# A decoder block whose attention computes its scores a second time with the keys as rows, instead of transposing the probabilities

## The chip, the cores and the metric

The kernel runs on one core of one Trainium2 chip. The metric is the device time of one execution in microseconds. Three runs of the kernel before gave a median of 816.69 us (815.62 to 818.06).

## The reference, cut to what matters

```
x = x + attn(layernorm(x))              # 4 x 512 x 512, 16 heads of 32, causal
x = x + xattn(layernorm(x), ctx, ctx)   # queries = layernorm(x), keys = values = ctx, causal
x = x + ffn(layernorm(x))
attn:  q, k, v = x @ w.T + b;  softmax(mask(q k' / sqrt(32))) @ v;  then @ o_w.T + o_b
ffn:   relu(x @ W_up.T) @ W_down.T + sum(softmax(top2(x @ W_gate.T))) * (x @ W_expert)
```

Everything is fp32. The softmax subtracts the largest score of its row.

## The kernel before, in words

Each engine runs one list of instructions, written out in the order of a loop over steps `s`; every step has 8 slots `i` (`z = 8 s + i`). A step handles one pair of heads. There are 32 pairs of self attention (4 batch entries of 8) and then 32 of cross attention; two pairs make a group `G` of four heads, 128 columns of the model. The order is the same on all engines, and engines meet through semaphores only.

Large matmuls are made exact enough by splitting each operand in a high and a low part (fp32r) and adding three products, lines 412 to 414. One such filling of a bank is 12 matmuls of 512 columns ("a fill"): Q, K of each group, V and O of each batch entry, and FG, FU, FE, FD of the feed-forward part. `plan` (line 91) lists the fills by slot, one quarter of a fill per slot, and gives each one of two banks. Fills of the feed-forward part of batch entry f begin at slot `FEED[f]`, steps 42.5, 51.5, 60 and 67.5.

For the scores the three products lie one above the other in a `stack` tile of 96 rows (32 numbers per head, three times), which SyncE fills by six DMAs per pair from `stage` (line 278), two steps ahead of use. Then, per pair, for each of two heads and each of four blocks of 128 queries:

- TensorE: `scores` (line 370), one matmul with queries as rows, 128 to 512 keys wide, because the mask is causal; three banks take turns.
- VectorE: `top_of` (line 558) adds the mask, scales, writes the tile to SBUF and takes the row's negative maximum.
- ScalarE: `exped` (line 770), the exponential with that maximum as bias and with the row sum accumulated.
- In self attention VectorE takes the reciprocal of four row sums (line 572) and GpSimd multiplies the tile by it (line 872).
- TensorE: `turn` (line 382), 20 transposes of 128x128 per pair, so that keys are rows; ScalarE (line 779) and VectorE (line 568) copy them out of two banks into `prob`.
- Every second step `values` (line 406): 16 matmul calls, each 32 columns of V against up to 512 columns of `prob`, four side by side in the array. Each call shows as two instructions.

In cross attention the division comes later: the result is transposed back (`back`, line 513) and multiplied by the reciprocal of the sums (`back_scaled`, line 681). At step s the engines work on the scores of pair s+1, the turning of pair s, and at even s the values of group s/2-1.

Of the kernel before, what the change touches and what calls it, by code (L numbers as in the profile page):

```python
# [59 lines left out]
FIRST = -4  # L60
# [5 lines left out]
NS, NTB = 3, 2  # L66


FEED = (PAIRS * 42 + 4, PAIRS * 51 + 4, PAIRS * 60, PAIRS * 67 + 4)


def feed_start(f):

    return FEED[f]


def stats_step(j):

    return PAIRS * (j - 1) + (2 if j == B + 2 else 0)


def norm_slots(j):

    z = PAIRS * PAIRS * (j - 1) + PAIRS * (2 if j < B else 3)
    return [z + 4, z + 5, z + 8, z + 9] if j == B + 2 else [z, z + 1, z + 4, z + 5]


END = (feed_start(B - 1) + UNITS) // PAIRS + 1


def plan():
# [6 lines left out]
    for G in range(NGS):  # L98
        put(("Q", G), 2 * G - 4, 4 if G and G % KC == 0 else 0, 4)
        put(("K", G), 2 * G - 3, 0, 4)  # L100
    for b in range(B):
        for t in range(NT):
            if b:
                put(("V", b, t), PAIRS * b - 3 + t, 4, 4)
                put(("L", b, t), PAIRS * b - 5, 5 + t, 1)
            else:
                put(("V", b, t), t - 2, 4, 4)
            if b == B - 1:
                put(("O", b, t), NPS + 1 + t // 2, 4 * (t % 2), 4)
            else:  # L110
                put(("O", b, t), PAIRS * (b + 1) + 1 + t, 4 if t < 2 else 0, 4)
    for f in range(B):
        u = feed_start(f)
# [10 lines left out]
    for z, slots, held, key in jobs:  # L124
        n = free.index(min(free))
        assert free[n] <= z
# [11 lines left out]
def decoder_block(nc, dram):  # L138
# [4 lines left out]
    with ExitStack() as ctx:  # L143
# [11 lines left out]
        h_hi, h_lo = w_hi[:, HID], w_lo[:, HID]  # L155
        xT_hi = sb("xT_hi", [PART, KC, T], F32R)
        xT_lo = sb("xT_lo", [PART, KC, T], F32R)
        stage = sb("stage", [PART, 2, 4, T], F32R)
        stack = sb("stack", [PART, 2, 2, 2, T], F32R)
        V = [sb("V0", [PART, NT, D]), sb("V1", [PART, NT, D])]  # L160
        xln = V[0]
        probs = sb("probs", [PART, 3, OFF[NT]])
        prob = [sb(f"prob{kb}", [PART, 4, T - PART * kb]) for kb in range(NT)]
        xt = sb("xt", [PART, NT, D])
        xres = sb("xres", [PART, NT, D])
        kraw = sb("kraw", [PART, 2, T])
        cn = sb("cn", [PART, T])
        row = sb("row", [PART, T])
        o_bias, lg = row, row
        ident = sb("ident", [PART, PART])  # L170
        mask = sb("mask", [PART, T])
# [3 lines left out]
        g_hi = sb("g_hi", [PART, KC, PART], F32R)  # L175
        g_lo = sb("g_lo", [PART, KC, PART], F32R)
        negmax = sb("negmax", [PART, 2, 2, NT])
        rowsum = sb("rowsum", [PART, 2, 2, NT])
        rsum = sb("rsum", [PART, 2, 2, NT])
        c_rowsum = sb("c_rowsum", [PART, 3, NT, 4])  # L180
        c_rsum = sb("c_rsum", [PART, 2, NT, 4])
        stats = sb("stats", [PART, NT, 6])
        mv = sb("mv", [PART, NT, 2])
        veps = sb("veps", [PART, NT])
        rstd = sb("rstd", [PART, NT])
        f_stats = sb("f_stats", [PART, NT, 6])
        f_mv = sb("f_mv", [PART, NT, 2])
        f_veps = sb("f_veps", [PART, NT])
        f_rstd = sb("f_rstd", [PART, NT])
# [4 lines left out]
        with nc.sbuf_tensor("cx", [PART, RING, 2, T], F32R) as cx:  # L194
# [4 lines left out]
        raw = [probs.rearrange("p h n -> p (h n)")[:, 0:KC * D].rearrange("p (c n) -> p c n", c=KC),  # L199
               prob[0], xres, V[1]]  # L200
        f_raw = {UP: f_xln, EXPERT: res2, DOWN: f_xln}

        s_bank = [bank(f"s{i}") for i in range(NS)]
        t_bank = [bank(f"t{i}") for i in range(NTB)]
        pv_bank = bank("pv")
        m_bank = [bank("m0"), bank("m1")]
        first_bank = [*m_bank, pv_bank, t_bank[0]]
# [8 lines left out]
        small_in, made = sem("small_in"), sem("made")  # L216
        g_loaded, g_cleared, g_hi_done, g_lo_done = sem("g_loaded"), sem("g_cleared"), sem("g_hi_done"), sem("g_lo_done")
# [3 lines left out]
        kraw_in = [sem("kraw_in0"), sem("kraw_in1")]  # L221
# [23 lines left out]
        def copied(P, i):  # L245

            if i in T_ACT:
                return t_act, len(T_ACT) * P + T_ACT.index(i) + 1
            return t_dve, len(T_DVE) * P + T_DVE.index(i) + 1
# [760 lines left out]
```

## Time and profile before

| | |
|---|---|
| median of 3 runs | 816.69 us |
| the profiled execution | 816.02 us |
| its span, first to last instruction | 814.1 us |
| TensorE busy with matmuls | 718.2 us (88%) |
| ScalarE, VectorE, GpSimd busy | 517.2, 505.9, 255.5 us |
| mean granted TensorE clock | 0.952 of 2.4 GHz |
| moved by DMA | 86.16 MB |

Busy time of TensorE is the union of its matmuls from issue to last result, so it holds some 0.17 us of pipeline behind each. In the rows by stretch below the columns are start:end and length in us, then the busy time (and number of instructions) of PE, PEld, DVE, ACT and POOL, the granted TensorE clock as a share of 2.4 GHz, the share of the DMA engines and their GB/s. Step 0 begins at 35.3 us, step 32 at 408.3, step 34 at 433.5, step 42 at 509.6, step 44 at 534.5 and step 64 at 749.4. What a matmul costs in a stream is the distance from its start to the next one's start.

### The profile page before, as it was taken

The page shows a single profiled execution, that of the slowest core. Times are in us where ns is not written, and L with a number is a line of the kernel's source. Part 1 is how long each engine was busy: PE and PEld are TensorE (multiplying, and loading weights), DVE is VectorE, ACT ScalarE, POOL GpSimd, SP SyncE. Part 2 cuts the span into 40 slices and gives each one's busy share as a digit, 9 for nine tenths or more (in the row PEclk, how much of TensorE's full clock was granted, in tenths as well). Part 3 has the DMA queues.
Part 4 walks back from the last instruction along what each step waited for, and adds up shares of the span by engine and source line. Part 5 has one row for each costly group of instructions (what it writes and reads, how often), then busy time and mean ns, then how long its engine had stood idle before and what let it go on. Part 6 is the DMA issues. An engine that isn't in the chain of part 4 may idle for free.

```text
span 814.1 us, 14482 instructions
## 1 busy us (share of the span) xinstructions
PE 718.2 (88%) x4480; PEld 538.7 (66%) x4480; DVE 505.9 (62%) x1726; ACT 517.2 (64%) x1450; POOL 255.5 (31%) x390
## 2 busy tenths in 40 slices
PE   4997998979989899897789776899987999899998
PEld 3765676757766677675557544677765777667776
DVE  5466557656566565756556667766778667664532
ACT  6567676657766577666756777677667776675020
POOL 3634343334444344534630573301021112000100
PEclk9998899999999999999779898799999999999999
DMA  9542433225433353225654676333435353420001
GB/s 320 121 130 54 115 79 79 60 67 159 115 69 79 91 167 93 65 67 143 197 140 96 190 200 156 73 91 91 127 88 144 85 132 76 120 51 1 18 35 52
DMA packets 45995, 86.16 MB, mean 106 GB/s; under 512 B 8416, under 2 KB 8416, under 8 KB 45920
## 3 DMA queue, kind: packets, MB, share of 16 engines
q1 hardware_dynamic: 45920, 85.25, 40.0%
q8 instruction: 36, 0.59, 0.3%
q14 instruction: 39, 0.32, 0.1%
HBM read 27.55 MB, written 7.34 MB: 43 GB/s over the span
## 4 chain that ended last, share of the span: by engine, by line
PE 66%; DVE 12%; issue 8%; ACT 8%; POOL 4%; DMA 1%; DVEq 0%; SPq 0%; POOLq 0%; ACTq 0%
PE t L382 14%; PE m L412 11%; PE m L413 11%; PE m L414 11%; PE pv L406 10%; PE s L370 6%; DVE probs L558 3%; ACT probs L770 3%; POOL probs L872 3%; ACT prob L779 2%; DVE stats L585 2%; DVE prob L568 1%; PE m L425 1%; POOL w_lo L912 1%; PE pv L513 1%
## 5 line engine op out<-in xcount | busy, mean ns | idle before, releaser
L770 ACT ACTIVATE probs<-probs,negmax 128x128 f32<-128x128 f32 (+3 forms) x512 | 286.1, 559 | 138.9 <-DVE negmax L558 132.7
L558 DVE CUSTOM_DVE_ANT_0 probs<-s,mask 128x128 f32<-128x128 f32 (+3 forms) x512 | 247.0, 486 | 170.5 <-PE s L370 168.1
L382 PE MATMUL t<-ident,probs 128*128 128x128 f32 x1280 | 240.3, 290 | 66.8 <-ACT prob L779 53.6
L382 PEld LDWEIGHTS t<-ident,probs 128*128 128x128 f32 x1280 | 162.7, 146 | 144.2 <-ACT prob L779 84.1
L370 PE MATMUL s<-stack 96*128 96x128 f32 (+3 forms) x512 | 207.4, 408 | 0.0
L872 POOL TENSOR_SCALAR probs<-probs,rsum 128x128 f32<-128x128 f32 (+3 forms) x256 | 132.4, 536 | 217.6 <-DVE rsum L572 212.0
L779 ACT ACTIVATE prob<-t 128x512 f32<-128x512 f32 (+1 forms) x256 | 135.6, 530 | 82.6 <-PE t L382 82.3
L568 DVE COPY prob<-t 128x256 f32<-128x256 f32 (+1 forms) x256 | 91.2, 356 | 28.6 <-PE t L382 27.7
L370 PEld LDWEIGHTS s<-stack 96*128 96x128 f32 x512 | 103.0, 201 | 7.5 <-issue 0.5
L770 ACT ACTIVATION_READ_ACCUMULATOR probs<-probs,negmax 128x1 f32 x512 | 96.3, 188 | 0.0
L406 PE MATMUL pv<-prob,V 128*32 128x512 f32 (+3 forms) x1024 | 83.4, 470 | 0.0
L412 PE MATMUL m<-xT_hi,w_lo 128*128 128x512 f32 x192 | 81.2, 423 | 0.9 <-DVE xT_lo L624 0.9
L413 PE MATMUL m<-xT_lo,w_hi 128*128 128x512 f32 x192 | 77.7, 405 | 0.0
L414 PE MATMUL m<-xT_hi,w_hi 128*128 128x512 f32 x192 | 77.4, 403 | 0.0
L406 PEld LDWEIGHTS pv<-prob,V 128*32 128x32 f32 x1024 | 31.4, 116 | 52.8 <-issue 46.5
L412 PE MATMUL m<-w_hi,xT_lo 128*128 128x512 f32 x128 | 52.5, 410 | 0.0
L413 PE MATMUL m<-w_lo,xT_hi 128*128 128x512 f32 x128 | 50.4, 394 | 0.0
L414 PE MATMUL m<-w_hi,xT_hi 128*128 128x512 f32 x128 | 50.3, 393 | 0.0
L908 POOL TENSOR_TENSOR res<-cn,res 128x512 f32<-128x512 f32 x8 | 10.5, 1314 | 118.9 <-DVE cn L681 118.9
L646 DVE SCALAR_TENSOR_TENSOR stage<-m,bias,stage 128x512 fp32r<-128x512 f32 x32 | 24.0, 751 | 33.9 <-ACT stage L809 33.9
L414 PEld LDWEIGHTS m<-xT_hi,w_hi 128*128 128x128 f32 x192 | 37.3, 194 | 8.9
L558 DVE DVE_READ_ACCUMULATOR2_ANT negmax<- 128x1 f32 x512 | 42.5, 83 | 0.0
(126 smaller groups left out, 902.1 us busy)
## 6 DMA issues: line engine op xcount, KB each, us to landing
stack<-stage SPq DMA_DIRECT2D x384, 128.0 KB, 2.3
xt<-in_x SPq DMA_DIRECT2D x16, 256.0 KB, 4.5
xres<-in_x SPq DMA_DIRECT2D x4, 1024.0 KB, 5.9
kraw<-in_ctxT SPq DMA_DIRECT2D x16, 256.0 KB, 2.9
V<-in_ctx SPq DMA_DIRECT2D x4, 1024.0 KB, 6.2
x<-xres SPq DMA_DIRECT2D x3, 1024.0 KB, 4.6
res<-x SPq DMA_DIRECT2D x8, 256.0 KB, 5.4
out<-res SPq DMA_DIRECT2D x2, 1024.0 KB, 4.4
```

What stands on the lines that cost most here:

```text
L370: nc.tensor.matmul(score_tile(P, i), stack[0:RS, P % 2, h, 0, chunk(qb)], stack[0:RS, P % 2, h, 1, 0:N], start=True, stop=True).then_inc(s ...
L382: mm = nc.tensor.transpose(dst[:, chunk(qb - kb)], probs[:, (2 * P + h) % 3, OFF[qb] + PART * kb:OFF[qb] + PART * kb + PART], ident[:, :])
L406: mm = nc.tensor.matmul(pv_bank[HD * j:HD * j + HD, PART * kb:T], v[:, kb, col:col + HD], prob[kb][:, j, :], start=(kb == 0), stop=(kb == ...
L412: nc.tensor.matmul(dst, lhs[1], rhs[0], start=(c == 0), stop=False)
L413: nc.tensor.matmul(dst, lhs[0], rhs[1], start=False, stop=False)
L414: return nc.tensor.matmul(dst, lhs[0], rhs[0], start=False, stop=(c == KC - 1))
L558: nc.vector.tensor_tensor_reduce(probs[:, (2 * P + h) % 3, OFF[qb]:OFF[qb + 1]], score_tile(P, i), mask[:, T - N:T], -SCALE, BIG, ALU.add, ...
L568: nc.vector.tensor_copy(prob[kb][:, 2 * (P % 2) + h, :], turned_tile(P, i)).then_inc(t_dve, 1)
L646: nc.vector.scalar_tensor_tensor(out=stage[:, n % 2, lo, :], in0=src[:, :], scalar=bias[:, w, n % KC:n % KC + 1], in1=f32(stage[:, n % 2, ...
L770: nc.scalar.activation(tile, tile, ACT.Exp, bias=negmax[:, P % 2, h, qb:qb + 1], scale=-1.0, accum_out=total).then_inc(p_exp, 1)
L779: nc.scalar.activation(prob[kb][:, 2 * (P % 2) + h, :], turned_tile(P, i), ACT.Copy).then_inc(t_act, 1)
L872: nc.gpsimd.tensor_scalar(tile, tile, rsum[:, P % 2, h, qb:qb + 1], 0.0, ALU.mult, ALU.add).then_inc(p_done, 1)
```

## The change: scores twice, sums by ones-matmuls

- The first score pass stays (`scores`), one step later in the loop (pair s at step s), with two banks instead of three. `top_of` now only serves to find the maximum: it writes back to PSUM.
- `split_max` splits four maxima per head in a high and a low part, `turn_max` transposes this small tile on TensorE into `x_bank`, `max_out` copies it to SBUF, and SyncE's `load_max` puts it as rows 96 and 97 into the stack's query side; the key side has ones there.
- `scores_turned` computes the scores again with keys as rows (98 rows of contraction), so that the maximum is subtracted in the matmul: 8 matmuls per pair in 5 tiles of exactly 512 columns. `exped` takes 5 full tiles straight from PSUM. GpSimd zeroes the half of each diagonal block above the diagonal (`cut`).
- The transposes of probabilities, the copies behind them, the row sums accumulated by ScalarE and GpSimd's multiplication of the tiles are gone.
- `values` runs on the undivided tiles, one step pair later (group s/2-2). `raw_values` copies the result to `cn`. `sums` runs the same matmuls with a tile of ones in place of V, in the same bank, for all groups (`PLAIN` is all). In self attention VectorE takes the reciprocal of the 128x512 sums in four parts, GpSimd multiplies and makes the low part, and ScalarE adds the bias. In cross attention the sums too are transposed back.
- `stack` has three buffers in place of two. The load for pair s+1 stands in step s, behind the second `load_max` of pair s-1, and waits for all turned scores of pair s-2.
- The fills of Q, K, V, O are spread evenly over the slots; normalization (`norm`, `f_norm`) goes from VectorE to ScalarE, with two more small GpSimd operations; the high part of the feed-forward weights goes from GpSimd to ScalarE; the gate uses 8 instead of 128 rows. `FEED` begins at steps 45, 53, 61, 69 and the loop at step -2 instead of -4.

The first `need` on `st_mm` below is the one added to `load_stack`.

```diff
-FIRST = -4
+FIRST = -2
-NS, NTB = 3, 2
+NS, NST = 2, 2
+TILE_SLOT = ((1, 3), (1, 5), (1, 7), (2, 1), (2, 2))
+MAX_SLOT = ((0, 5), (1, 1))
+PLAIN = range(0, NG)
+FEED = tuple(PAIRS * (NPS + 13 + PAIRS * f) for f in range(B))
...
-        put(("Q", G), 2 * G - 4, 4 if G and G % KC == 0 else 0, 4)
-        put(("K", G), 2 * G - 3, 0, 4)
+            put(("Q", G), PAIRS * c, (-3, 9, 25, 44)[k] if G > 1 else -8, 4, 3)
+            put(("K", G), PAIRS * c, (1, 17, 32, 51)[k], 4, 3)
...
+                need(sp, st_mm, TILES * (P - RP + 1))
...
+            def load_max(P, h):
+                sp.wait_ge(mx_out, 2 * P + h + 1)
+                need(sp, st_mm, TILES * (P - RP + 1))
+                sp.dma_start(f32(stack[RS:XS, P % RP, h, 0, :]), f32(mxT[0:2 * NT, h, :])).then_inc(mx_in[P % RP][h], 16)
...
+            def scores_turned(P, j):
+                if j in (0, 2):
+                    pe.wait_ge(mx_in[P % RP][j // 2], 16 * (P // RP + 1))
+                need(pe, p_exp, TILES * P + j - NST + 1)
+                for h, kb in parts(j):
+                    at = place(h, kb)[1]
+                    mm = nc.tensor.matmul(turned_bank(P, j)[:, at:at + T - PART * kb], stack[0:XS, P % RP, h, 1, chunk(kb)],
+                                          stack[0:XS, P % RP, h, 0, PART * kb:T], start=True, stop=True)
+                mm.then_inc(st_mm, 1)
...
+            def sums(G):
+                pe.wait_ge(cn_done, G + 1)
+                if G in PLAIN:
+                    for kb in range(NT):
+                        for j in range(4):
+                            mm = nc.tensor.matmul(pv_bank[HD * j:HD * j + HD, PART * kb:T], ones[:, :],
+                                                  prob_of(2 * G + j // 2, j % 2, kb), start=(kb == 0), stop=(kb == NT - 1))
...
-                    if 0 <= s + 1 < NP:
-                        scores(s + 1, i)
+                    if 0 <= s < NP:
+                        scores(s, i)
                     for key, part in RUNNING.get(z, ()):
                         fill(key, part)
-                    if s % 2 == 0 and 0 <= s // 2 - 1 < NG and i == 0:
-                        for kb in range(NT):
-                            values(s // 2 - 1, kb)
-                    if 0 <= s < NP:
-                        turn(s, i)
+                    if s % 2 == 0 and 0 <= s // 2 - 2 < NG and i == 0:
+                        values(s // 2 - 2)
+                    if s % 2 == 0 and 0 <= s // 2 - 2 < NG and i == 3:
+                        sums(s // 2 - 2)
+                    for j, (later, slot) in enumerate(TILE_SLOT):
+                        if i == slot and 0 <= s - later < NP:
+                            scores_turned(s - later, j)
+                    for h, (later, slot) in enumerate(MAX_SLOT):
+                        if i == slot and 0 <= s - later < NP:
+                            turn_max(s - later, h)
...
+            def recip(G, q):
+                if q == 0:
+                    dve.wait_ge(sum_mm, G + 1)
+                    need(dve, cn_scaled, G)
+                nc.vector.reciprocal(rs[:, chunk(q)], pv_bank[:, chunk(q)]).then_inc(r_done, 1)
...
+                nc.scalar.activation(PT[:, P % RP, j, :], turned_bank(P, j)[:, :], ACT.Exp, scale=SCALE).then_inc(p_exp, 1)
...
+            def cut(P, j):
+                pool.wait_ge(p_exp, TILES * P + j + 1)
...
+                nc.gpsimd.affine_select(out=tile, in_=tile, compare_op=ALU.is_ge, fill=zero, base=0,
+                                        pattern=[[0, len(parts(j))], [1, PART]], channel_multiplier=-1).then_inc(p_cut, 1)
```

In VectorE's list `split_max` of the first head stands at slot 4 of the pair's step and that of the second at slot 0 of the next one; `recip` stands at slots 4 to 7 of even steps.

## Rows read from the trace of the kernel before

**Rows 1.** The page's first part: busy time, share and instructions of each engine.
```profile
PE 718.2 (88%) x4480; PEld 538.7 (66%) x4480; DVE 505.9 (62%) x1726; ACT 517.2 (64%) x1450; POOL 255.5 (31%) x390
```

**Rows 2.** The page's chain that ended last: shares of the span by engine.
```profile
PE 66%; DVE 12%; issue 8%; ACT 8%; POOL 4%; DMA 1%; DVEq 0%; SPq 0%; POOLq 0%; ACTq 0%
```

**Rows 3.** Busy time by stretch: before step 0; steps 2-32; 34-42; 44-64; rest.
```profile
0.00:35.30 35.30, 23.68 (x96) 19.59 (x97) 17.42 (x42) 19.25 (x38) 15.46 (x22) 1.00 0.74 231
57.50:408.30 350.80, 312.82 (x1974) 232.41 (x1973) 212.28 (x762) 237.52 (x669) 149.13 (x264) 0.95 0.39 100
433.50:509.60 76.10, 58.75 (x410) 39.48 (x413) 50.43 (x183) 55.61 (x168) 34.41 (x37) 0.90 0.64 165
534.50:749.40 214.90, 200.90 (x1360) 153.50 (x1359) 149.59 (x515) 149.29 (x430) 30.24 (x30) 0.98 0.37 93
751.70:814.10 62.40, 57.75 (x265) 46.91 (x261) 23.03 (x46) 6.07 (x11) 2.56 (x3) 1.00 0.09 34
```

**Rows 4.** TensorE in order of time, one slot with transposes: start, us, what.
```profile
38.51 0.49 PE L382 MATMUL t<-ident,probs 128*128 128x128 f32 x3
38.76 0.42 PE L370 MATMUL s<-stack 96*128 96x384 f32 x1
39.01 0.40 PE L412 MATMUL m<-xT_hi,w_lo 128*128 128x512 f32 x1
...
39.72 0.38 PE L382 MATMUL t<-ident,probs 128*128 128x128 f32 x2
```

**Rows 5.** TensorE in order of time, scores without transposes around them.
```profile
30.09 0.34 PE L370 MATMUL s<-stack 96*128 96x384 f32 x1
30.27 0.40 PE L412 MATMUL m<-xT_hi,w_lo 128*128 128x512 f32 x1
...
30.96 0.40 PE L370 MATMUL s<-stack 96*128 96x512 f32 x1
31.20 0.40 PE L412 MATMUL m<-xT_hi,w_lo 128*128 128x512 f32 x1
```

**Rows 6.** TensorE in order of time, one group's values and what follows.
```profile
57.48 2.36 PE L406 MATMUL pv<-prob,V 128*32 128x512 f32 x32
59.77 0.66 PE L382 MATMUL t<-ident,probs 128*128 128x128 f32 x4
```

**Rows 7.** Groups by shape: busy us in all, mean ns of one, idle before.
```profile
L779 ACT ACTIVATE prob<-t 128x512 f32<-128x512 f32 x128 | 75.0, 586 | 78.4 <-PE t L382 78.4
L558 DVE CUSTOM_DVE_ANT_0 probs<-s,mask 128x512 f32<-128x512 f32 x128 | 88.0, 687 | 5.9 <-PE s L370 5.6 <-issue 0.3
L568 DVE COPY prob<-t 128x128 f32<-128x128 f32 x128 | 37.1, 290 | 4.4 <-PE t L382 4.2
L572 DVE RECIPROCAL rsum<-rowsum 128x4 f32<-128x4 f32 x64 | 11.1, 173 | 0.0
L576 DVE RECIPROCAL c_rsum<-c_rowsum 128x16 f32<-128x16 f32 x16 | 3.9, 243 | 0.0
L699 DVE TENSOR_TENSOR gap<-top 128x4 f32<-128x4 f32 x4 | 0.7, 166 | 0.1
L932 POOL TENSOR_SCALAR_AFFINE_SELECT mask<-mask 128x128 f32<-128x128 f32 x1 | 0.3, 292 | 0.0
```

**Rows 8.** The page's costliest groups: mean over the shapes of a line.
```profile
L558 DVE CUSTOM_DVE_ANT_0 probs<-s,mask 128x128 f32<-128x128 f32 (+3 forms) x512 | 247.0, 486 | 170.5 <-PE s L370 168.1
L770 ACT ACTIVATE probs<-probs,negmax 128x128 f32<-128x128 f32 (+3 forms) x512 | 286.1, 559 | 138.9 <-DVE negmax L558 132.7
L872 POOL TENSOR_SCALAR probs<-probs,rsum 128x128 f32<-128x128 f32 (+3 forms) x256 | 132.4, 536 | 217.6 <-DVE rsum L572 212.0
```

**Rows 9.** SyncE's stack loads: issue min/median/max ns in one stretch, and their time to landing there.
```profile
L290 SPq DMA_DIRECT2D stack<-stage x16: 559/604/611, 469.6 to 489.4; - x16
...
DMA to landing us min/median/max: 2.3/4.3/6.7
```

**Rows 10.** The page's DMA issues: count, KB each, median us to landing, whole span.
```profile
stack<-stage SPq DMA_DIRECT2D x384, 128.0 KB, 2.3
```

More of the change, by code:

```diff
@@ L839, in _ @@
                     split_hi(i, c)
+            act.wait_ge(made, 6)
+            for r in range(RP):
+                for h in range(2):
+                    nc.scalar.activation(stack[RS:XS, r, h, 1, :], ones[RS:XS, 0:1].broadcast_to([XS - RS, T]), ACT.Copy)\
+                        .then_inc(ones_row, 1)
             act.wait_ge(small_in, 64)
@@ L850, in _ @@
                             empty(key)
-                    if 0 <= s + 1 < NP:
-                        exped(s + 1, i)
-                    if 0 <= s < NP and i in T_ACT:
-                        turned(s, i)
-                    if s % 2 == 0 and 0 <= s // 2 - 1 < NG and i == 3:
-                        context_hi(s // 2 - 1)
-                    if s % 2 == 1 and NGS <= (s + 3) // 2 < NG and i == 2:
+                    for h, (later, slot) in enumerate(MAX_SLOT):
+                        if i == slot + 1 and 0 <= s - later < NP:
+                            max_out(s - later, h)
@@ new lines, in _ @@
+                    if s % 2 == 0 and 0 <= s // 2 - 2 < NG and i == 2:
+                        raw_values(s // 2 - 2)
+                    for j, (later, slot) in enumerate(TILE_SLOT):
+                        if i == slot and 0 <= s - later < NP:
+                            exped(s - later, j)
+                    if s % 2 == 0 and NGS <= s // 2 - 2 < NG and i == 4:
+                        raw_sums(s // 2 - 2)
+                    if s % 2 == 1 and 0 <= (s - 5) // 2 < NGS and i == 2:
+                        context((s - 5) // 2)
@@ L858, in _ @@
+                    if s % 2 == 1 and NGS <= (s + 3) // 2 < NG and i == 4:
                         query_hi((s + 3) // 2)
+                    for j in range(1, 2 * B):
+                        if z in norm_slots(j):
+                            norm(j, norm_slots(j).index(z))
                     for f in range(B):
-                        if z == feed_start(f) + TURN_AT + 3:
+                        if 0 <= z - f_norm_slot(f) < NT:
+                            f_norm(f, z - f_norm_slot(f))
+                        if z == FEED[f] + TURN_AT + 3:
@@ L976, in _ @@
-                if 0 <= s + 1 < NPS:
-                    for qb in range(NT):
-                        scaled(s + 1, 0, qb)
+                    if 0 <= s - SPLIT_AT[n] < KC:
+                        f_split_lo(n, slot, s - SPLIT_AT[n])
 def kernel(**inputs):
```

618 lines of the change are left out of this document (345 added, 273 removed).

## The prediction

> **What bounds the kernel now.** I read the busy shares first, then the chain of waits, then the busy times by stretch, and last TensorE's instructions one by one. The shares show TensorE at 88% and two engines above 60% [rows 1]. The chain that ended last runs 66% over TensorE and 12% and 8% over VectorE and ScalarE [rows 2]. So TensorE bounds most of it, but not alone. The stretches say where. In steps 2 to 32 (350.8 us, 11.7 us a step) TensorE is at 89% by its union of matmuls; in steps 34 to 42, attention with next to no fills, it has 58.8 of 76.1 us (9.5 us a step), the DMA engines are 0.64 busy, and ScalarE has 55.6 of 76.1; in steps 44 to 64, with the feed-forward fills, 200.9 of 214.9; in the last stretch fills are all there is [rows 3].
>
> The union flatters TensorE, so I count distances from start to start. A fill matmul takes 0.23 us (39.01 to 39.72 is three of them), a fill of 12 so 2.8 us. One slot with transposes, 38.51 to 39.72, costs 1.21 us, of which 0.70 is fill and 0.25 each three transposes and a 384-wide score [rows 4]. Where no transposes stand around it the same 384-wide score costs 0.18 us and the 512-wide one 0.24 us [rows 5]: behind a row of short transposes some 0.07 us of the weight load lies bare. A pair's scores and turning take 8 x 0.43 = 3.4 us (I take the 0.50 of that slot less 0.07 for the slots with one or two transposes). The values of a group run from 57.48 to 59.77, 2.29 us, 1.15 a pair [rows 6]. Attention is thus 4.6 us a step in self attention, and 5.0 in cross attention with two sets of four transposes of some 0.35 us every second step.
>
> Steps 0 to 32 hold 54 fills (Q and K 14 each, V 14, O 12): 32 x 4.6 + 54 x 2.8 + 4 (layer norm transposes) = 302 us of the 373 between 35.3 and 408.3. So 19% of that time TensorE starts nothing; in the feed-forward steps it is 5.0 + 37.8/8.3 = 9.6 of 10.7 us, 11%.
>
> **TensorE, after.** Removed: 20 transposes per pair, and with them the bare weight loads of the scores. What stays of a head's scores is 0.12 + 0.12 + 0.18 + 0.24 = 0.66 us, 1.3 a pair [rows 5]. Added: turned scores of the same 2560 columns; the trace has none with 98 rows. Nearest are the scores without transposes, 1.3 us a pair; the bound above is the scores with transposes (each 0.07 dearer, 1.9), below the columns alone, 5 x 0.21 = 1.05. I take 1.3. Added: `sums`, the same columns as the values, hence 2.29 us a group or 1.15 a pair [rows 6]; no bound is needed, since columns, types and column tiles are those of `values`. Added: two small transposes of maxima, 0.09 each by the transposes (0.25 for three), 0.2 a pair. Attention becomes 1.3 + 1.3 + 1.15 + 1.15 + 0.2 = 5.1 us (I carry 5.2 for the changes of tile size) in self and 5.2 + 0.36 + 0.18 = 5.7 in cross attention, where the sums are transposed back too. That is 0.6 to 0.7 more a step than before: the transposes go, and the ones-matmuls give it back and more. In all TensorE's stream grows by 64 x 0.65 = 42 us. A gain can only come from the 140 us or so in which TensorE now starts nothing.
>
> **ScalarE.** Removed: 8 exponentials of 559 ns mean [rows 8], 8 accumulator reads, and four copies of the turned tiles, 586 ns the widest [rows 7]. Added: 5 exponentials of 512 columns from PSUM. The copy of that shape has 586 ns, 2.9 a pair; the bound above is the exponential of 128x512 at the slope of the mean row, 0.75, or 3.7. Two copies of maxima (0.2 to 0.3 each), raw values and context (1.6 a group), and the norms that VectorE gives up. It was 237.5/30 = 7.9 us a step [rows 3] and comes to 5.9 or less. ScalarE leaves the bound, and with it the chain s_max, exponential, GpSimd, transposes, copy that ends in TensorE: this is the real gain.
>
> **VectorE.** `top_of` stays, 8 x 486 ns plus accumulator reads, 4.5 us a step [rows 8]; PSUM instead of SBUF as its target I cost at nothing: the source already is PSUM (bounds -0.05 to +0.1 us each, -0.4 to +0.8 a step, which VectorE's spare 1.5 us a step hides; without that cover it would be 26 us at most). The copies go, 1.4 a pair (290 ns for 128 columns [rows 7]). `split_max` adds four small ones at 0.17 [rows 7], 0.7. The new reciprocals are 128x128 from PSUM, four a group. Rows: 173 ns for 4 columns, 243 ns for 16 [rows 7], 5.8 ns a column, so 0.9 us each, 1.8 a step. Below, a copy of 128 columns has 0.29 us; above, if all of the 243 ns were per column, 1.9 us. I take 0.9. VectorE's step in self attention: 4.5 + 0.7 + 1.8 + 0.75 (Q, K) + 0.5 (O, norm transposes) + 0.4 (statistics) = 8.7 us against TensorE's 10.2. The Trainium skill (VectorE: DVE Perf Modes, The DVE is not a fixed-function vector unit, note on slices) says reciprocal runs iterative divide steps with a repeat count of 8; if that were eight cycles a column at its 0.96 GHz, an estimate from that page is 1.2 us each and 2.4 a step, and with 1.3 in place of 1 us on each even step the sum would be 5 us later than mine. The two rows bear out a cost per column far above a copy's.
>
> The reciprocals stand at slots 4 to 7 of even steps, in front of `split_max` of the second head at slot 0, for which TensorE waits at slot 1 (`turn_max`). From the last score matmul TensorE has about 3.4 us of other work until there; VectorE has a backlog of 1.5, the 512 tile 0.77, a reciprocal 0.9, an emptying 0.75, the next tile 0.37 and the split 0.35: 4.6 or more. I charge 1 us on each of 16 even steps, 16 us.
>
> **GpSimd** loses 4 x 536 ns a head, 4.3 a pair [rows 8], and gets five cuts, 292 ns for 128 columns [rows 7], 1.9 a pair, and 1.3 for dividing and low part: hidden, it was idle for 217.6 us before its old multiplications alone [rows 8].
>
> **SyncE and the stack.** It issues at 0.60 us a DMA [rows 9]; six loads and two of the maxima are 4.8 us a step. Before, a load had nearly two steps; now it starts when pair s-2 has its last turned tile (slot 2 of step s) and is wanted at slot 0 of step s+1. To there: one load of maxima 0.6, three of the first head 1.8, landing 2.3 in the median [rows 10], but 4.3 in steps 36 to 40, where weights and residuals come in too, up to 6.7 [rows 9]. That is 4.7 to 6.7 us. TensorE has six slots: 7.7 us with fills, enough; without fills 4.3, too little. Slots 0 to 2 of the next step add 1.3 to 3.6. So a step without fills takes 7.0 to 9.3 us whatever TensorE has to do. I take 8.3, one less than now.
>
> **The sum**, against the profiled execution (span 814.1 us, 1.9 less than its time of 816.02, which lies 0.7 below the median of the runs):
> - to step 0: 35 us, as now (two steps less, but the same Q, K and weights must be there) [rows 3].
> - steps 0 to 32: 56 fills x 2.8 + 32 x 5.2 + 4 = 327; 6% lost, as in the best two-step stretches before, 347; reciprocals 16: 363 (now 373). At 398.
> - steps 32 to 45: 13 x 8.3, and the last four O fills half hidden, 6: 114. At 512.
> - steps 45 to 66: 5.7 + 37.8/8 = 10.4, 6% lost, 11.1: 233. At 745.
> - rest: four feed-forward parts are 151 us, 99 done, 52 left, 3 of gap before the last, 3 of emptying and storing: 58. At 803.
> With the 1.9 us around it: 805 us.
>
> **Rivals.**
> - TensorE is kept full: the reciprocals never stop it and light steps go at 6.5 us. For it: the fills are spread evenly and ScalarE is light. Against it: two score banks instead of three couple VectorE and TensorE more closely. 805 - 16 - 13 x 1.8 + 8 (a rest of both) = 774.
> - Slower: the reciprocal is near its upper bound. Then VectorE has 4.5 + 0.7 + 3.8 + 1.65 = 10.7 us a step against TensorE's 10.2. It decides from 1.6 us a reciprocal, where both are equal. With 11.9 us a step as it comes with 10% lost, steps 0 to 32 take 381: 823 us. For it: four small pieces rather than one long instruction. Against: the slope of the two rows.
> - Slower: the late stack loads and maxima set the pace of all cross attention, at 9.3 us without fills and 12 with: 13 + 19 more, 837 us. For it: 0.64 DMA share and landings of 4.3 us there [rows 3, 9].
> - Nothing: the 42 us of matmuls eat what the idle time gives, 816.
>
> **How the numbers follow.** A measurement of this kernel can tell 0.3%, 2.4 us. My forecast, 805 with its own range 792 to 818, has 0.42; full TensorE 0.20; reciprocals 0.15; loads 0.12; nothing gained 0.11. Faster is the second, most of the first (0.39) and a little of the last: 0.60. Same 0.10, the rest slower, 0.30. The range reaches to half of the rivals at either end: 774 to 836.
>
> **What would show it.** Right: `scores_turned` at 0.24 us a tile from start to start, `sums` at 2.3 us a group, TensorE's stream 710 to 720 us, ScalarE's busy below 400 us, step 32 near 398. Reciprocals at 0.9 us. Waits of TensorE at `turn_max` behind even steps, and of score matmuls for stack loads in steps 34 to 45. Wrong: reciprocals above 1.5 us, steps of 32 to 45 at 6.5 or above 9.3, landings of the maxima above 4 us, turned scores much dearer than the first pass.

## The result, and where the time went

The changed kernel takes 870.39 us (median of 4 runs, 865.85 to 872.94), the kernel before 816.67 beside it: ratio 1.065, 95% interval 1.060 to 1.070. The forecast was 805, with a range up to 836: wrong in sign and size.

The page of the changed kernel, busy shares and then the first row of its chain, against [rows 1] and [rows 2]:

```profile
PE 760.9 (87%) x4928; PEld 529.4 (61%) x4928; DVE 521.9 (60%) x1666; ACT 364.5 (42%) x728; POOL 272.9 (31%) x497
...
PE 64%; DVE 17%; issue 8%; ACT 6%; DMA 3%; SPq 2%; POOL 1%; DVEq 0%; POOLq 0%; ACTq 0%
```

TensorE's busy time grows by 42.7 us, where its stream was said to grow by 42, and ScalarE loses 153 us. Both look as forecast, though the first is partly luck: with the same matmuls and copies in place of the reciprocals (e2 below) TensorE's busy time is 748.5 us, so some 12 of the 42.7 us belong to the stops and the clock and not to the stream. But VectorE's share of the chain rises from 12% to 17%. The 140 us or so in which TensorE starts nothing were to shrink to 88 (803 less a stream of 715, the middle of 710 to 720). They grew instead: the span grew by 57.1 us, 14 more than TensorE's busy time.

Busy time by stretch, columns as in [rows 3]: before step 0; steps 4 to 32; 32 to 36; 36 to 45; 45 to 66; rest. Steps 4, 32, 36 and 66 begin with a group's values; step 45 has no values and is put midway between steps 44 and 46 (its first score starts at 566.5).

```profile
0.00:36.00 36.00, 20.69 (x83) 16.43 (x84) 17.46 (x38) 18.99 (x32) 16.04 (x24) 0.95 0.78 248
65.10:424.70 359.60, 314.21 (x2046) 219.52 (x2047) 232.36 (x688) 153.05 (x304) 104.94 (x193) 0.95 0.35 90
424.70:474.60 49.90, 36.78 (x221) 21.79 (x220) 32.72 (x103) 20.86 (x43) 27.66 (x42) 0.73 0.57 162
474.60:564.50 89.90, 76.54 (x565) 47.67 (x565) 55.38 (x207) 42.36 (x88) 39.30 (x72) 0.91 0.50 128
564.50:802.30 237.80, 225.25 (x1588) 158.34 (x1587) 143.06 (x513) 104.39 (x218) 72.04 (x144) 1.00 0.35 89
802.30:871.20 68.90, 60.36 (x306) 44.76 (x305) 20.19 (x42) 9.59 (x16) 3.00 (x5) 0.92 0.08 31
```

Steps 4 to 32 take 12.8 us a step, where steps 2 to 32 took 11.7 [rows 3]. VectorE is busy for 8.3 us of each (232.36 / 28). By its sum it should never have been the bound. The kernel before, whose groups come one step pair earlier, spent 332.1 us on the same 14 groups: 297.9 busy on TensorE and 34.2 idle, against 314.2 and 45.4 here. So of the 57.1 us that the span grew by, 27.5 lie here, 6.0 in the next four steps, none in the ten after those (36 to 46), 11.8 in steps 46 to 66, 7.6 before the first values and 4.2 in the rest.

What ended TensorE's waits in the kernel before, then in the changed one (waiter, line, releaser; us, times, longest):

```profile
PE t L382 <- ACT prob L779: 53.6, 70, 1.8
...
PE t L382 <- DVE prob L568: 7.0, 12, 1.3
```

```profile
DVE s L639 <- PE s L416: 246.4, 262, 4.2
...
PE s L416 <- DVE negmax L639: 37.5, 63, 2.0
PE xb L438 <- DVE mx L648: 27.5, 30, 2.6
```

The wait for ScalarE's copies (and VectorE's) of the turned tiles, 61 us, is gone as forecast. A wait for VectorE took its place, 65 us. Meanwhile VectorE waited 246 us for TensorE's scores (168 before [rows 8]). Two engines that wait for each other and are both far from full: one even step in order of time shows how. TensorE, the changed kernel, 202 to 214 us (fills left out):

```profile
202.67 2.36 PE L470 MATMUL pv<-PT,ones 128*32 128x512 f32 x32
204.96 0.50 PE L428 MATMUL st<-stack 98*128 98x512 f32 x1
205.30 0.23 PE L416 MATMUL s<-stack 96*128 96x128 f32 x1
...
211.65 0.40 PE L428 MATMUL st<-stack 98*128 98x384 f32 x2
213.58 0.27 PE L438 MATMUL xb<-ident,mx 128*8 128x128 f32 x1 [1.53 <-DVE mx L648]
213.61 0.42 PE L416 MATMUL s<-stack 96*128 96x384 f32 x1
```

VectorE and one row of GpSimd in the same time:

```profile
202.83 0.69 DVE L728 TENSOR_TENSOR xres<-m,xres 128x512 f32<-128x512 f32 x1
205.71 0.30 DVE L639 CUSTOM_DVE_ANT_0 s<-s,mask 128x128 f32<-128x128 f32 x1 [2.19 <-PE s L416]
205.93 0.14 DVE L639 DVE_READ_ACCUMULATOR2_ANT negmax<- 128x1 f32 x1
205.93 0.17 DVE L646 CAST mx<-negmax 128x4 fp32r<-128x4 f32 x1
...
206.21 0.96 DVE L655 RECIPROCAL rs<-pv 128x128 f32<-128x128 f32 x1
207.09 0.41 DVE L639 CUSTOM_DVE_ANT_0 s<-s,mask 128x256 f32<-128x256 f32 x1
207.41 0.14 DVE L639 DVE_READ_ACCUMULATOR2_ANT negmax<- 128x1 f32 x1
207.41 0.95 DVE L655 RECIPROCAL rs<-pv 128x128 f32<-128x128 f32 x1
...
210.86 0.94 DVE L655 RECIPROCAL rs<-pv 128x128 f32<-128x128 f32 x1
211.73 0.27 DVE L639 CUSTOM_DVE_ANT_0 s<-s,mask 128x128 f32<-128x128 f32 x1
211.92 0.14 DVE L639 DVE_READ_ACCUMULATOR2_ANT negmax<- 128x1 f32 x1
211.92 1.26 DVE L646 CAST mx<-negmax 128x4 fp32r<-128x4 f32 x1
213.21 0.32 DVE L648 TENSOR_TENSOR mx<-negmax,mx 128x4 fp32r<-128x4 f32 x1
```

```profile
211.89 1.26 POOL L1011 TENSOR_TENSOR cn<-cn,rs 128x512 f32<-128x512 f32 x1 [0.72 <-DVE rs L655]
```

While TensorE runs the sums (2.3 us, and the values before them), it makes no score tile and VectorE starves (2.19). Then the group's four reciprocals fall due at once, between four maxima, and from 205.71 to 213.4 VectorE is busy without a gap. TensorE, with two score banks, can be two tiles ahead and no more, and it stops at the maxima of the second head (1.53). The two take turns: that is the reading that the experiments test. And the cast just before, 0.17 us at 205.93, takes 1.26 us at 211.92, beside a GpSimd instruction of 1.26.

### The profile page after: what moved, and what is told of

Its sections match the earlier page's. It is cut to its first block, busy times and chain, and to the rows that moved or that the text cites. A ratio compares the mean times of both kernels' runs of the same rounds, so it can differ in the third digit from the quotient of the medians.

```text
span 871.2 us, 15146 instructions
## 1 busy us (share of the span) xinstructions
PE 760.9 (87%) x4928; PEld 529.4 (61%) x4928; DVE 521.9 (60%) x1666; ACT 364.5 (42%) x728; POOL 272.9 (31%) x497
## 4 chain that ended last, share of the span: by engine, by line
PE 64%; DVE 17%; issue 8%; ACT 6%; DMA 3%; SPq 2%; POOL 1%; DVEq 0%; POOLq 0%; ACTq 0%
PE m L484 10%; PE m L485 9%; PE m L486 9%; PE pv L460 9%; PE pv L470 8%; PE s L416 7%; PE st L428 7%; DVE s L639 5%; DVE rs L655 4%; DVE mx L646 2%; PE xb L438 2%; ACT f_xln L863 1%; DVE negmax L639 1%; DMA stack<-stage 1%; PE m L497 1%
## 5 line engine op out<-in xcount | busy, mean ns | idle before, releaser
L639 DVE CUSTOM_DVE_ANT_0 s<-s,mask 128x128 f32<-128x128 f32 (+3 forms) x512 | 251.2, 496 | 248.1 <-PE s L416 246.4
L825 ACT ACTIVATE PT<-st 128x512 f32<-128x512 f32 x320 | 190.5, 596 | 389.8 <-PE st L428 388.6
L989 POOL TENSOR_SCALAR_AFFINE_SELECT PT<-PT 128x256 f32<-128x256 f32 (+1 forms) x320 | 115.4, 362 | 457.0 <-ACT PT L825 456.9
L428 PE MATMUL st<-stack 98*128 98x512 f32 (+3 forms) x512 | 139.0, 334 | 0.0
L428 PEld LDWEIGHTS st<-stack 98*128 98x128 f32 x512 | 99.8, 203 | 21.5 <-issue 6.1
L460 PE MATMUL pv<-PT,V 128*32 128x512 f32 (+3 forms) x1024 | 82.8, 468 | 0.0
L470 PE MATMUL pv<-PT,ones 128*32 128x512 f32 (+3 forms) x1024 | 75.6, 436 | 2.7 <-ACT cn L873 2.7
L438 PE MATMUL xb<-ident,mx 128*8 128x128 f32 x128 | 36.1, 282 | 30.2 <-DVE mx L648 27.5
L655 DVE RECIPROCAL rs<-pv 128x128 f32<-128x128 f32 x64 | 60.9, 951 | 0.0
L484 PEld LDWEIGHTS m<-xT_hi,w_lo 128*128 128x128 f32 x192 | 37.4, 195 | 13.1 <-DVE stage L721 4.4
```

The costliest lines, as they stand in the source:

```text
L428: mm = nc.tensor.matmul(turned_bank(P, j)[:, at:at + T - PART * kb], stack[0:XS, P % RP, h, 1, chunk(kb)], stack[0:XS, P % RP, h, 0, PART ...
L438: nc.tensor.transpose(x_bank[0:2 * NT, 0:PART], f32(mx[:, h, :, :]).rearrange("p i n -> p (i n)"), ident[:, :])\
L460: mm = nc.tensor.matmul(pv_bank[HD * j:HD * j + HD, PART * kb:T], v[:, kb, col:col + HD], prob_of(2 * G + j // 2, j % 2, kb), start=(kb == ...
L470: mm = nc.tensor.matmul(pv_bank[HD * j:HD * j + HD, PART * kb:T], ones[:, :], prob_of(2 * G + j // 2, j % 2, kb), start=(kb == 0), stop=(k ...
L484: nc.tensor.matmul(dst, lhs[1], rhs[0], start=(c == 0), stop=False)
L639: nc.vector.tensor_tensor_reduce(score_tile(P, i), score_tile(P, i), mask[:, T - N:T], -1.0, BIG, ALU.add, ALU.min, negmax[:, P % 2, h, qb ...
```

## The experiments

Each was timed beside the kernel before, on the same chip. Stages are taken from the profiled run, from the values of one group to those of another; for the kernel before they are the stages of the same groups, steps 2 to 30, 30 to 44 and 44 to 64. What each run changes is told below.

```
run                    us      ratio [95%]            4-32    32-46  46-66  rest
before                 816.7   1                      332.1   144.9  215.0  64.7
after                  870.4   1.065 [1.060, 1.070]   359.5   150.9  226.8  68.9
e2 copies for recips   826.6   1.014 [1.008, 1.019]   319.4   148.9  227.0  68.4
e4 sums short          844.5   1.033 [1.030, 1.036]   344.5   150.8  214.7  67.1
e6 narrow maxima       852.9   1.044 [1.042, 1.047]   343.5   148.9  224.7  68.2
e7 recips spread       848.8   1.039 [1.036, 1.043]   337.1   149.6  226.3  69.1
d1 e2 and e4           803.0   0.983 [0.981, 0.985]   306.7   146.1  216.2  68.0
d2 e7 and e4           814.3   0.998 [0.996, 1.001]   318.4   152.1  215.0  67.0
d3 e2, e4 and e6       785.4   0.960 [0.957, 0.964]   298.4   142.7  213.5  67.2
g2 d3, two loads       775.9   0.953 [0.950, 0.955]   297.5   136.0  210.7  67.3
```

**Two score banks instead of three.** The changed kernel has two; are they what couples the engines? The kernel before, with two score banks (b1, first line added), and again with the freed bank given to the turned tiles (b2, the other):

```diff
-NS, NTB = 3, 2
+NS, NTB = 2, 2
...
+NS, NTB = 2, 3
```

> The kernel before with two score banks in place of three, nothing else. Theory A (VectorE's round trip): with two banks TensorE waits for the maximum of the tile before last, as the changed kernel does, so this alone costs 10 us or more (826 to 845 us). Theory B (TensorE's own stream of matmuls, 42 us longer, is what the change costs): the third bank is worth little, under 4 us (under 821 us).

811.0 us, ratio 0.9945 [0.992, 0.997].

> The kernel before with two score banks and three banks for the turned tiles. With two and two it was 0.55% faster than before, and TensorE's waits at the transposes for ScalarE's copies had fallen from 138 to 80 us, its waits at the scores risen from 0 to 64. If the free bank lengthens the queue where the transposes wait, it gains 5 to 20 us (790 to 806 us). If ScalarE's own time is the bound in those steps, it stays at 808 to 814 us.

810.4 us, 0.991 [0.988, 0.994]: with b1 the only complete kernels here that beat the one before, and the third turned bank adds nothing that can be told from b1. TensorE's waits in b1:

```profile
PE s L370 <- DVE negmax L558: 27.7, 44, 1.5
PE t L382 <- ACT prob L779: 26.8, 54, 1.7
```

A wait for maxima appears (27.7 us), and as much goes from the wait for the copies (53.6 before). In the kernel before, two banks are no loss, so the bank by itself does not explain the 54 us. What a third one would give the changed kernel was not tried. Why b1 gains 5 us was not settled; two of the 13 runs of the kernel before beside it took 810.5 and 811.8 us as well.

**The reciprocals' work.** Left out: the division in self attention.

```diff
-                nc.vector.reciprocal(rs[:, chunk(q)], pv_bank[:, chunk(q)])
+                nc.vector.tensor_copy(rs[:, chunk(q)], pv_bank[:, chunk(q)])
```

> The changed kernel with the 64 reciprocals of 128x128 replaced by copies of the same tiles, so the self attention is not divided by its sums. It takes 64 x 0.66 = 42 us from VectorE, all in steps 4 to 34. Theory A: VectorE paces that stretch, and 15 to 35 us of it come back (835 to 855 us). Theory B: less than 4 us.

826.6 us, 43.8 less, for 42.6 us of work (64 x (951 - 286 ns)), although VectorE is 60% busy. More than the 15 to 35 us expected. The instruction, changed kernel and then this one:

```profile
L655 DVE RECIPROCAL rs<-pv 128x128 f32<-128x128 f32 x64 | 60.9, 951 | 0.0
```

```profile
L655 DVE COPY rs<-pv 128x128 f32<-128x128 f32 x64 | 18.3, 286 | 0.0
```

Steps 4 to 32, changed kernel's row above, here:

```profile
65.80:385.30 319.50, 300.64 (x2045) 213.29 (x2044) 189.48 (x688) 151.54 (x304) 104.73 (x193) 0.98 0.40 101
```

Of the 40.1 us, 26.5 are idle time of TensorE (45.4 to 18.9); 13.6 are busy time, for the same matmuls, with the mean granted clock at 0.98 instead of 0.95. (At most 5 of the 13.6 are the 0.17 us that the union counts behind each stop, 53 stops against 25.) So as much came back as the work left out, but not because every part of it was waited for: a stop comes with more than its length, and the cast fell as well, from 317 to 220 ns, with fewer meetings of the kind tested by e1 below (VectorE's busy time is 47 us less, not 42.6).

**Their place.** Spread over slots 5, 6 of the even step and 1, 2 of the odd one:

```diff
-                    if s % 2 == 0 and 0 <= s // 2 - 2 < NGS and i >= 4:
-                        recip(s // 2 - 2, i - 4)
+                    if s % 2 == 0 and 0 <= s // 2 - 2 < NGS and i in (5, 6):
+                        recip(s // 2 - 2, i - 5)
+                    if s % 2 == 1 and 0 <= (s - 5) // 2 < NGS and i in (1, 2):
+                        recip((s - 5) // 2, i + 1)
```

(and `context` from slot 2 to slot 6)

> The changed kernel with the four reciprocals of a group at slots 5 and 6 of the even step and slots 1 and 2 of the odd one, in place of slots 4 to 7 of the even step (ScalarE's context three slots later for it). VectorE does the same work. Theory D (only their place, ahead of the second head's split_max, costs): 10 to 25 us come back (845 to 860 us). Theory A' (VectorE lacks the time as such): under 6 us, since copies in their place gave back 44 us for 42 us of VectorE.

848.8 us, 21.6 less, with the same instructions. Half of the reciprocals' cost is where they stand (with `context`, which had to move too).

**On ScalarE,** which is busy for 157 us less than VectorE now, as exp(-ln x):

```diff
+                nc.scalar.activation(rs[:, :], pv_bank[:, :], ACT.Ln).then_inc(ln_of, 1)
+                act.wait_ge(ln_of, G + 1)
+                nc.scalar.activation(rs[:, :], rs[:, :], ACT.Exp, scale=-1.0).then_inc(r_done, NT)
...
-                    if s % 2 == 0 and 0 <= s // 2 - 2 < NGS and i >= 4:
-                        recip(s // 2 - 2, i - 4)
```

> The changed kernel with the reciprocal of the sums made by ScalarE, as exp(-ln(sum)) in two instructions of 512 columns, in place of VectorE's four. ScalarE is busy only 42% of the span and gets 16 x (1.2 us and the loads of the two tables, 2 x 1.3). Theory A': VectorE loses all 61 us of reciprocals, and the time falls by 30 to 60 us (810 to 840 us). Against: ScalarE holds up the exponentials of the next pair while its tables change, then 840 to 860 us.

871.3 us, 1.064 [1.059, 1.069]: no gain, and outside both expectations. VectorE's busy time fell by 55 us (521.9 to 466.8); each group pays two table loads on ScalarE instead:

```profile
L886 ACT ACT_TABLE_LOAD x16 | 20.5, 1283 | 0.3
L888 ACT ACT_TABLE_LOAD x16 | 20.5, 1283 | 1.2
```

With the two activations that is 3.8 us in one piece on ScalarE, behind which emptyings and exponentials queue: VectorE's Q and K low parts wait 37.0 us for `stage`, 13.4 in the changed kernel.

**The standstill.** GpSimd's 512-wide tensor_tensors, each in four pieces of 128 columns (one of six shown):

```diff
-                nc.gpsimd.tensor_tensor(cn[:, :], cn[:, :], rs[:, :], ALU.mult).then_inc(cn_scaled, 1)
+                for q in range(NT):
+                    op = nc.gpsimd.tensor_tensor(cn[:, chunk(q)], cn[:, chunk(q)], rs[:, chunk(q)], ALU.mult)
+                op.then_inc(cn_scaled, 1)
...
```

> The changed kernel with GpSimd's tensor_tensor of 512 columns each cut into four of 128 columns. In the trace the small cast of VectorE took 1.26 us instead of 0.17 exactly while GpSimd ran such an instruction. Theory C (VectorE stands still behind a GpSimd tensor_tensor, at the place where TensorE waits for the maxima): the cast is held 0.35 us at most and the time falls 6 to 15 us (855 to 864 us). Theory B: no change, 868 to 873 us.

862.1 us, 8.3 less, net: the pieces also make GpSimd's work 38 us longer (310.7 against 272.9). The cast, changed kernel and then this one (busy us, mean ns):

```profile
L646 DVE CAST mx<-negmax 128x4 fp32r<-128x4 f32 x128 | 40.5, 317 | 0.1
```

```profile
L646 DVE CAST mx<-negmax 128x4 fp32r<-128x4 f32 x128 | 30.6, 239 | 0.1
```

**The target of the maxima.** `top_of` writes into SBUF again:

```diff
-                nc.vector.tensor_tensor_reduce(score_tile(P, i), score_tile(P, i), mask[:, T - N:T],
+                nc.vector.tensor_tensor_reduce(acc.rearrange("p a b n -> p (a b n)")[:, OFF[qb]:OFF[qb + 1]], score_tile(P, i), mask[:, T - N:T],
```

> The changed kernel with top_of writing its tile to spare SBUF instead of back to the PSUM bank. The instruction and its accumulator read were 10 and 57 ns dearer than before, 34 us of VectorE in all, and each lies in the round trip score, maximum, next score but one. Theory A: the read falls back to 83 ns and the time by 8 to 25 us (845 to 862 us). Theory B: under 3 us.

864.8 us, 5.6 less, below the 8 expected at least and hardly clear of the spread (864.4 to 871.5, the changed kernel 865.9 to 872.9). The instructions themselves lost 36 us: the read of the accumulator fell from 140 to 83 ns, and the maximum from 496 to 482. VectorE's busy time fell by 20, since a read runs beside what follows it and the subtraction grew:

```profile
L639 DVE DVE_READ_ACCUMULATOR2_ANT negmax<- 128x1 f32 x512 | 71.9, 140 | 0.1
```

```profile
L639 DVE DVE_READ_ACCUMULATOR2_ANT negmax<- 128x1 f32 x512 | 42.5, 83 | 0.1
...
L648 DVE TENSOR_TENSOR mx<-negmax,mx 128x4 fp32r<-128x4 f32 x128 | 37.0, 289 | 4.4
L646 DVE CAST mx<-negmax 128x4 fp32r<-128x4 f32 x128 | 24.2, 189 | 0.1
```

(first fence: changed kernel). The standstill did not go, it moved: the cast fell from 317 to 189 ns and the subtraction behind it rose from 192 to 289.

**TensorE's sums.** Over the first key block alone (left out: three of four key blocks):

```diff
-                    for kb in range(NT):
+                    for kb in range(1):
...
```

> The changed kernel with the sums taken over the first of the four key blocks only (4 matmul calls a group in place of 16, so the sums are incomplete): 1.37 us of TensorE less in each of 32 groups, 44 us. Theory B (the longer stream of TensorE is what the change costs): 35 to 44 us come back (826 to 835 us). Theory A (VectorE's tiles in slots 4 to 7 of the even steps pace it): those begin when the block of sums ends, so part comes back in both cases, but where VectorE lags the time is its own: 20 to 44 us, and no less in self than in cross attention.

844.5 us: 26 of 44 us of TensorE's work come back. By stage, at 1.37 us a group: 15.0 of 19.2 in steps 4 to 32, 12.1 of 13.7 in steps 46 to 66, and 0.1 of 9.6 in the light steps between, those with few fills. And key blocks added up on GpSimd first, one block for TensorE:

```diff
-PLAIN = range(0, NG)
+PLAIN = range(NG, NG + 1)
...
```

> The changed kernel with the key blocks of all groups added up by GpSimd first (three tensor_tensor per pair, 3.8 us) and the ones-matmuls run on block 0 and the added tile: 1.37 us of TensorE a group less, exactly as in the kernel with short sums, but with 240 us more of GpSimd. Theory B: as fast as with short sums. Theory C (VectorE stands still while GpSimd runs a tensor_tensor): slower than with short sums by 20 us or more, perhaps slower than the changed kernel itself (870).

900.1 us, 1.101 [1.098, 1.104]; as few columns for the sums as in e4, 56 us slower. VectorE's busy time rises from 521.9 to 563.5 us for the same instructions. The small operations, mean 474 and 347 ns:

```profile
L646 DVE CAST mx<-negmax 128x4 fp32r<-128x4 f32 x128 | 60.7, 474 | 0.1
L648 DVE TENSOR_TENSOR mx<-negmax,mx 128x4 fp32r<-128x4 f32 x128 | 44.5, 347 | 4.4
```

**The maxima's work,** over the first 128 keys alone (left out: the maximum over the others):

```diff
-                nc.vector.tensor_tensor_reduce(score_tile(P, i), score_tile(P, i), mask[:, T - N:T],
+                N = PART
+                nc.vector.tensor_tensor_reduce(score_tile(P, i)[:, 0:N], score_tile(P, i)[:, 0:N], mask[:, 0:N],
```

> The changed kernel with top_of taking only the first 128 keys of every tile (the maximum is then over a part of the row). VectorE loses 512 x 0.2 = 102 us, in self and cross attention alike, and nothing else changes. Theory A': 50 to 80 us come back (790 to 820 us), the light steps 36 to 44 fall from 10 to 8 us each. Theory E (cross attention is paced by stack loads and landings of the maxima): little comes back from step 34 on, under 5 us, all of it before.

852.9 us: 17.5 for some 100 us of VectorE's work, where e2 gave 43.8 for 42.6. The 50 to 80 us expected did not come: 16.0 came in steps 4 to 32, and in the light steps 36 to 46 nothing (100.6 us against 100.9). Work that is spread over all slots lies mostly beside TensorE's; work that comes in one piece does not.

**Together.** c1 is e1, e3 and e7 in one; c2 is c1 with e2's copies.

> The changed kernel with three edits together: GpSimd's tensor_tensor in four pieces, top_of writing to SBUF, the reciprocals spread over both steps. Alone they gave 8, 6 and 22 us. If each takes time from the same wait (TensorE for VectorE's split maxima) the sum is less than the parts: 842 to 850 us. If they lie in different places of VectorE's list they add up: 832 to 840 us. Neither reaches the kernel before (816).

849.7 us, as e7 alone.

> The same three edits, and copies in place of the reciprocals (self attention is not divided by its sums). Theory A' (VectorE's time ahead of TensorE's waits is what the change costs beyond my sum): with all four taken away the forecast's 805 us is reached, 800 to 815 us. Theory B: it stays above 820, because TensorE's longer stream and the light steps cost the rest.

833.8 us, 7.2 more than e2 alone. Steps 4 to 32 take the same (319.2 and 319.4); the loss lies in steps 36 to 46, 107.6 us against 101.1. TensorE now waits 9.4 us in all for `cx` from GpSimd, whose pieces or later `context` may be in the way; which of them was not tried. Do gains never add? The next three say when they do (d1: e2 and e4; d2: e7 and e4; d3: e2, e4 and e6).

> Copies in place of the reciprocals and sums over the first key block only (left out: the division by the sums in self attention, and three of four key blocks of every sum). Alone the first gave 826.6 and the second 844.5 us, from 870.4. Theory T, taking turns: in an even step TensorE runs values and sums while VectorE starves, and then VectorE runs maxima and reciprocals while TensorE waits two score tiles ahead; each is on the path in its own part, so the two gains add: 870.4 - 43.8 - 25.9 = 801 us (795 to 808). Rival F, a floor elsewhere (stack loads, ScalarE, the half clock that idle time brings): the combination of moved reciprocals, copies and pieces stayed at 834, so this one stays at 815 or above.

803.0 us (taking turns said 801).

> Reciprocals kept, but spread over slots 5, 6, 1 and 2 as in the run that gave 848.8 us, and sums over the first key block only (left out: three of four key blocks of every sum), which alone gave 844.5 us. Theory T, taking turns: the spread shortens VectorE's part and the short sums TensorE's, the gains add: 870.4 - 21.6 - 25.9 = 823 us (816 to 830). Rival F: VectorE's work of a step is the same in both, so once TensorE's part is short VectorE's own sum of about 9.3 us a step bounds it, and the spread is worth nothing: 840 to 845 us.

814.3 us, below what taking turns said (823, range 816 to 830) and far from the rival's 840 to 845: 56 us for two parts that gave 48 alone. They do more than add; why was not settled.

> As the first of these three runs, and the maxima over the first 128 keys only (left out beside the division and three key blocks of the sums: the maximum over the other keys). VectorE loses another 100 us, its busy time falls below 390 us. Theory T: with both of VectorE's loads gone its part of the step is shorter than TensorE's, TensorE alone bounds, and the rest of the loss is what it waits for elsewhere; alone the maxima gave 17.5 us, but part of that is what the copies give already: 780 to 795 us. Rival F: no further gain over the first of the three (within 4 us), and steps 36 to 46 stay at 100 us, as they did in every run so far.

785.4 us (780 to 795 was expected by taking turns). A saving in TensorE's turn and one in VectorE's turn add. Of several in VectorE's turn some add and some don't: the narrow maxima are worth 17.6 us on top of d1 and 17.5 alone, while c1 is no better than e7. But steps 36 to 46 stay at 100.4 us (changed kernel 100.9). There, in d3, TensorE in order of time, a stretch by the columns of [rows 3], and SyncE in order of time:

```profile
441.08 0.79 PE L428 MATMUL st<-stack 98*128 98x512 f32 x1 [2.20 <-DMA stack<-mxT]
442.58 0.47 PE L416 MATMUL s<-stack 96*128 96x128 f32 x1 [0.70 <-DMA stack<-stage]
442.98 4.33 PE L460 MATMUL pv<-PT,V 128*32 128x512 f32 x32
```

```profile
441.00:446.60 5.60, 4.82 (x26) 1.77 (x30) 0.55 (x4) 0.60 (x1) 0.29 (x1) 0.50 0.36 96
```

```profile
433.14 0.66 SPq L333 DMA_DIRECT2D stack<-mxT  x1
433.90 1.76 SPq L313 DMA_DIRECT2D res<-x  x4
435.76 0.66 SPq L333 DMA_DIRECT2D stack<-mxT  x1
436.53 3.85 SPq L327 DMA_DIRECT2D stack<-stage  x6
```

SyncE issues from 433.14 to 441.14 without a gap. TensorE's wait for the maxima issued at 435.76 ends only at 441.08; it has stood for 2.20 us by then, and behind that stop the values run at a granted clock of 0.50, the lower of the two levels, 1.2 GHz: 32 instructions in 4.33 us, where they take 2.36 at 2.4 GHz. So two loads a head instead of three in cross attention (left out: the third), in the changed kernel (g1) and in d3 (g2):

```diff
+                        if r < 2 or P < NPS:
+                            sp.dma_start(f32(stack[HD * r:HD * r + HD, P % RP, h, :, :]), f32(src[:, pick, :]))\
...
```

> The changed kernel, with two stack loads a head instead of three in cross attention (left out: the third, so that a third of each score there comes from old data). Five light steps' worth of it: SyncE loses 2 of 8 issues a step, 1.2 us, and the stacks land earlier. Theory S, the loads are one of three things that each take about 10 us of a light step (TensorE with VectorE, the stacks, the maxima's way back), and in the changed kernel they are not the last: steps 36 to 46 stay at 98 to 101 us, the whole gains at most 4 us, 866 to 872. Rival L, the loads set the light steps in the changed kernel too (my forecast said so): 36 to 46 fall to 90 or less, the whole to 858 or less.

869.3 us, no change clear of the spread; steps 36 to 46 at 97.9.

> The run with copies for reciprocals, short sums and narrow maxima (785.4 us, its steps 36 to 46 took 100.4 us as in every run), and two stack loads a head in cross attention (left out what those two leave out). Theory S: with VectorE unloaded the stacks come last in the light steps, so fewer loads shorten them: 36 to 46 fall to 85 to 93 us, the whole to 770 to 778. Rival C, the half clock and TensorE's own chain set the light steps whatever the loads do: 98 to 101 us, the whole within 3 us of 785.

775.9 us, 9.5 less than d3; steps 36 to 46 at 93.7, just above the 85 to 93 expected. The loads bound the light steps only once VectorE and the sums are out of the way. In the changed kernel no single part does: e2, e4, e6 and g1 leave these steps at 101.1, 102.3, 100.6 and 97.9 us. What else holds them was not tried.

## Why the prediction was wrong

The step that failed is the charge for the reciprocals: "I charge 1 us on each of 16 even steps, 16 us". Measured: 40 us in steps 4 to 32 (359.5 against 319.4), 2.9 us for each of 14 even steps (the last two groups' reciprocals fall in steps 32 and 34). Of the 2.9, 1.9 is idle time of TensorE; the other 1.0 is longer busy time behind the stops, for which the sum had no term. From step 0 to 32 the forecast had 363 us; it became 388.7. Without the reciprocals' work it would have been 347, and e2 has 349 (65.9 - 36 + 319.4). The rest of that sum came out within 2 us.

- TensorE's pieces were right: 5.25 us of attention a step (steps 14 and 15: of 24.63 us, 12.6 are their 54 fill matmuls and 1.5 waiting) where 5.2 stood; a turned tile 0.24 from start to start, as forecast; the sums 2.3 us a group (202.67 to 204.96).
- ScalarE was right in size, 364.5 us, and wrong in worth. "This is the real gain" named the wait that goes and not the one behind it: 61 us went, 65 came.
- The reciprocal was right: 951 ns, 0.9 forecast. So the slower rival fell too: its mechanism was a reciprocal of 1.9 us that makes VectorE's sum the larger. VectorE's sum stayed at 8.3 us (8.7 forecast) of 12.8. The error was to compare two sums of a step, and to charge only the reciprocal next to the one split that TensorE waits for, where each engine's work comes in a lump while the other has two tiles to go on. The four lumps of 0.95 us and the 4.6 us of values and sums stand in one even step, one behind the other. The Trainium skill (VectorE: DVE Perf Modes, First, the fixed hardware budget) gives a repeat count of 8 for the reciprocal's divide; an estimate of eight cycles a column at that page's 0.96 GHz is 8.3 ns. From 248 ns at 16 columns (the changed kernel's `c_rsum`, also read from PSUM) to 951 at 128 the trace shows 6.3 ns a column, and the measurement decides.
- "13 x 8.3" for the light steps failed as well, by as much (25.8 us): ten of them took 100.9 us, 10.1 each, and steps 32 to 46 took 150.9 where 125 was forecast (114 and one of 11.1). The 8.3 came from stack loads that leave TensorE idle. It was busy for most of the time and hardly waited for a load; its row for steps 36 to 46, and its waits for stack loads in the whole run:

```profile
474.60:575.50 100.90, 84.60 (x616) 53.65 (x615) 64.47 (x237) 51.36 (x106) 44.34 (x81) 0.92 0.49 123
```

```profile
PE s L416 <- DMA stack<-stage: 0.9, 2, 0.7
```

  Steps 32 to 36 have next to no fills; they took 49.9 us at a granted clock of 0.73, where 39 stood (4 x 8.3 + 6). So the rival of the late loads, 9.3 us a light step, comes near the time but not by its cause. What sets the pace of the light steps in the changed kernel stays open. The kernel before took 101 us for its ten from 34 to 44; I had looked at 34 to 42. The feed-forward part starts at step 45 instead of 42.5, so there are more of them.
- Late steps, 11.1 forecast, 11.3 measured. The rest was 68.9 instead of 58, and 67 to 69 in every run: I counted work still to do after step 66 too short; the gap before the last part, 4.3 us, was foreseen as 3.
- Not in the sum: the standstill (8.3 us by e1). PSUM as a target of the maxima, costed "at nothing", is some 5.6 us by e3, hardly clear of the spread and inside its bound of 26.

By stage: 1 + 25.7 + 25.8 + 4.8 + 10.9 = 68.2 us between the forecast's 803 and the span of 871.2.

## What to carry to other kernels

When two engines hand tiles to each other through two buffers, do not only compare their sums over a step; lay both out in time and look at what each does while the other runs its longest block. Work added to the less busy engine in one lump, just behind the other's lump, can cost all of itself (here 43.8 us for 42.6); spread out it cost half. And when a wait goes, find out which engine will end the next one before booking the gain.

## What the runs showed of the hardware

- A VectorE cast of 4 columns in SBUF takes 0.17 us, and 1.26 beside a GpSimd tensor_tensor of 1.26; in the changed kernel the 18 of 128 casts that begin while a 512-column one runs take 1.21 us in the mean, the others 0.17. The maxima and reciprocals, which read PSUM, show no such thing: 10 reciprocals that begin beside one take 0.95 us, as the other 54 do. The Trainium skill (SBUF — State Buffer, SBUF: two separate sides) says that a port pair shared by VectorE and GpSimd is held by one of them for its whole instruction; the trace agrees, and e1 gives the price here, 8.3 us; of e5's 56 us it is a part.
- The accumulator read after a maximum takes 140 ns where the maximum wrote to PSUM, 83 where it wrote to SBUF.
- Idle time of TensorE comes with longer busy time: in steps 4 to 32, against e2, 13.6 us more of it came with 26.5 us of idle time, at a mean clock of 0.95 instead of 0.98.
- A Ln between exponentials on ScalarE costs two table loads of 1283 ns, one before the Ln and one before the next Exp: 32 of them, 41 us, in e8.
